# Expert blocks in one region of rows: full blocks of the first half, a mixed block an expert, then the rest

## What is computed

```
x = x + tanh(g_xattn[0]) * attention(layernorm(x), ctx)          # layer 1, 16 heads of 8
x = x + tanh(g_ffn[0])   * moe0(layernorm(x))                    # layer 2, the blocks of this change
x = x + tanh(g_xattn[1]) * bidaf_attention(layernorm(x), ctx)    # layer 3, called C here
x = x + tanh(g_ffn[1])   * moe1(layernorm(x))                    # layer 4, called D here

def moe0(x, Wg, W1, W2, W3):            # E = 8 experts, top 2
    top_w, top_i = top_k(x @ Wg, 2); top_w = softmax(top_w)
    y_e = (silu(x @ W1[e]) * (x @ W2[e])) @ W3[e]                # 128 -> 256 -> 128
    out = sum over the two chosen experts of top_w * y_e
```

## Time and profile before

| | |
|---|---|
| time, median of 3 runs | 523.1 us (522.99 to 526.55) |
| the profiled execution: its time, and the span of its trace | 524.74 us, 523.0 us |
| mean granted TensorE clock | 0.990 |
| busy: PE, DVE, ACT, POOL | 486.1, 401.3, 316.0, 230.5 us |
| stage A, B, C and D of the first and second half | to 212, to 354, to 523 us |
| blocks in stage B | 80 |

### The profile page before, as it was taken

The page is one execution under the profiler, slowest core; times in us unless marked ns, Lnnn a source line. Parts: engine busy times, 40 slices in busy tenths (PEclk is TensorE's granted clock), DMA queues, the critical chain, the costliest instruction groups (busy, mean ns, idle before and its releaser), DMA issues. The chain is left out here.

```text
span 523.0 us, 14426 instructions
## 1 busy us (share of the span) xinstructions
PE 486.1 (93%) x4456; PEld 395.8 (76%) x4456; DVE 401.3 (77%) x1582; ACT 316.0 (60%) x777; POOL 230.5 (44%) x316
## 2 busy tenths in 40 slices
PE   2688999999999999999999999989998999899997
PEld 1366777777777777777888887866897878779897
DVE  5788888888889878767756677676699895777973
ACT  1567887777887776455566655556553557453553
POOL 3322155555454554532450656532468863224420
PEclk9999999999999999899999999998999999998999
DMA  8703011111001220155664443320000112000011
GB/s 243 291 11 93 12 42 37 36 35 36 30 30 32 63 63 21 51 141 166 206 190 120 127 125 106 95 68 20 21 23 26 50 42 66 12 0 2 2 42 40
DMA packets 48130, 36.86 MB, mean 70 GB/s; under 512 B 6466, under 2 KB 43970, under 8 KB 47812
## 3 DMA queue, kind: packets, MB, share of 16 engines
q1 hardware_dynamic: 31332, 21.13, 13.5%
q0 software_dynamic: 4640, 9.45, 6.3%
q10 hardware_dynamic: 12096, 5.51, 3.8%
HBM read 22.44 MB, written 13.63 MB: 69 GB/s over the span
## 5 line engine op out<-in xcount | busy, mean ns | idle before, releaser
L468 POOL DMA_INDIRECT sent<-xr,rowu x60 | 59.8, 996 | 52.1 <-DVE rowu L1037 26.8
L484 POOL DMA_INDIRECT yg<-done,gidx x64 | 64.2, 1003 | 41.7 <-PE bank L1629 17.4
L1663 PE MATMUL bank<-QK 128*64 128x256 f32 x512 | 70.5, 397 | 8.4 <-ACT QK L612 5.4
L443 POOL TENSOR_TENSOR ve<-mv,half 128x4 f32<-128x4 f32 (+1 forms) x40 | 8.9, 222 | 114.8 <-DVE mv L833 113.8
L1234 DVE TENSOR_TENSOR act<-sil,bank 128x256 f32<-128x256 f32 x80 | 33.6, 420 | 33.4 <-ACT sil L674 33.0
L624 ACT ACTIVATE PT<-bank 128x512 f32<-128x512 f32 x64 | 36.4, 602 | 33.2 <-PE bank L1629 32.4
L674 ACT ACTIVATE sil<-bank 128x256 f32<-128x256 f32 x80 | 30.8, 385 | 38.7 <-PE bank L1819 38.3
L1663 PEld LDWEIGHTS bank<-QK 128*64 128x64 f32 x512 | 32.2, 139 | 27.0 <-ACT QK L612 6.8
L1835 PE MATMUL bank<-f0w_s,aT 128*128 x320 | 50.1, 279 | 0.9 <-DVE yb L1240 0.6
L912 DVE TENSOR_REDUCE mx<-bank 128x8 f32<-128x512 f32 x64 | 43.9, 686 | 8.5 <-PE bank L1663 8.4
L916 DVE TENSOR_TENSOR Pr<-bank,mx 128x512 f32<-128x512 f32 x64 | 43.7, 683 | 1.6
(11 more groups left out here) (241 smaller groups left out, 1294.3 us busy)
## 6 DMA issues: line engine op xcount, KB each, us to landing
xb<-sent SPq DMA_DIRECT2D x80, 64.0 KB
done<-yb ACTq DMA_DIRECT2D x80, 64.0 KB
cT<-ctx_t_dram SPq DMA_DIRECT2D x16, 128.0 KB, 2.2
f0w_s<-f_w_dram SPq DMA_DIRECT2D x1, 2048.0 KB, 11.0
Pr<-ctx_t_dram SPq DMA_DIRECT2D x8, 256.0 KB
QK<-ctx_tok_dram SPq DMA_DIRECT2D x8, 256.0 KB
out_dram<-xs SPq DMA_DIRECT2D x8, 256.0 KB, 2.3
xs<-x_dram SPq DMA_DIRECT2D x2, 512.0 KB, 5.6
```

The lines of the kernel that those rows point to most:

```text
L468: nc.gpsimd.indirect_dma_start(sent, bass.IndirectOffsetOnAxis(ap=rowu[:, s, 2 * k + c:2 * k + c + 1], axis=0), rows[:, c, :], None).then_ ...
L484: nc.gpsimd.indirect_dma_start(yg[:, s, j, :], None, done[u // (U4 // HALVES)], bass.IndirectOffsetOnAxis(ap=gidx[:, s, j:j + 1], axis=0)) ...
L1663: last = mm(bank[g % 2][L * b:L * (b + 1), 256 * p:256 * (p + 1)], QT[:, s, g, t:t + L], Kb[:, s, :, t:t + L], start=True, stop=True)
```

## The change

Both halves now send into one set of regions, and there is one list of `NB` = 64 + 8 - 1 = 71 blocks. The first `NBF` = 32 - 7 = 25 can only be full blocks of the first half and need only its rows. Then come the other full blocks of the first half, one mixed block for each expert (the rest of the first half and what follows of the second), and the rest of the second half. Results of the first half are all within blocks 0 to 39 (`NBH` = 40 stays as that bound).

- The table of the first 25 blocks is made in stage A, from counts rounded down. The table of the other 46 is made in steps 6 to 18 of stage B from sums over 24 runs of blocks (8 full, 8 mixed, 8 rest).
- `run` is no longer set anew for the second half. `zero_after` is gone from POOL; there is one set of 8 tails, written by SyncE, one in each of the steps t = 16 to 23 of its loop, after `first_of(t + 1)`.
- `half_sent(1)` stands ahead of block 25, not 40, and waits for the early spare blocks (8, were 16) and the 8 tails.
- The words of the second table are needed from `NW` = 16: by `load_word` at step 20.
- The sends of the last two units are tied to blocks 8 to 15.
- The context loads move from t = 10 to 40 to t = 22 to 52.
- The `back_...` work is over 16 thresholds in place of 8 experts, 32 x 16 = 512 elements, at steps 19 to 28, with a new `back_first` twice.
- Gathers are tied to `b_xt` >= 45 + 7 i / 8, at most 71; `comb` begins at t = 53 and takes a unit every 8 steps (56 and 9 before). The start of layer 3 is three steps nearer to the end of the loop.

```diff
-REGION = TOKENS // HALVES + P
+REGION = TOKENS + P
-NBH = 2 * TOKENS // HALVES // P + E
-NB = HALVES * NBH
-NW = NBH - 3
+PAIRS = 2 * TOKENS // P
+NB = PAIRS + E - 1
+NBF = PAIRS // HALVES - (E - 1)
+NBH = PAIRS // HALVES + E
+NW = NBF - PACK + 1
+NS = 3 * E
+TAIL = 16
+CTX = 22
+COMB = 53
...
             def half_sent(h):
-                sp.wait_ge(zeroed, 16 * E * HALVES)
-                sp.wait_ge(S("tails"), 16 * E * (h + 1))
+                if h == 1:
+                    sp.wait_ge(zeroed, 16 * E * 2)
...
+            def zero_after(e):
+                sp.wait_ge(S("tail"), 1)
+                r = sp.value_load(tail[0:1, e:e + 1], min_val=e * REGION, max_val=e * REGION + TOKENS)
+                sp.dma_start(sent[bass.ds(r, P), :], zero[:]).then_inc(zeroed, 16)
...
             for t in range(4, NB):
-                if t == NBH:
+                if t == NBF:
                     half_sent(1)
                     r = first_of(t)
                 sp.wait_ge(S("b_xt"), t - 3)
                 b_load(t, r)
-                if t + 1 < NB and t + 1 != NBH:
+                if t + 1 < NB and t + 1 != NBF:
                     r = first_of(t + 1)
-                if 10 <= t < 10 + 4 * U4 and t % 4 == 2:
-                    c_columns((t - 10) // 4)
+                if TAIL <= t < TAIL + E:
+                    zero_after(t - TAIL)
+                if CTX <= t < CTX + 4 * U4 and t % 4 == 2:
+                    c_columns((t - CTX) // 4)
...
-                        pool.wait_ge(S("b_xt"), NBH + 5 + 35 * (8 * u + j) // 32)
+                        pool.wait_ge(S("b_xt"), min(NBH + 5 + 7 * (8 * u + j) // 8, NB))
...
-            send(UA - 2, 0, (9, 11, 13, 15))
-            send(UA - 1, 1, (17, 19, 21, 23))
-            zero_after(1)
+            send(UA - 2, 0, (8, 9, 10, 11))
+            send(UA - 1, 1, (12, 13, 14, 15))
...
-            fetch(2, range(2))
             rstd(2, 0, 4)
-            fetch(2, range(2, 8))
-            fetch(3, range(1))
+            fetch(2, range(8))
             rstd(2, 1, 4)
-            fetch(3, range(1, 8))
+            fetch(3, range(8))
             rstd(2, 2, 4)
...
+                if t == 6:
+                    t_runs()
+                    t_run_rows()
+                if t == 9:
+                    t_run_steps()
                 if t == 11:
-                    t_count(1)
+                    t_all()
                 if t == 12:
-                    t_blocks()
-                    t_ends()
+                    t_rest()
                 if t == 13:
-                    t_owner(1)
-                    t_expert(1)
+                    t_rest_sums()
                 if t == 14:
-                    t_before()
-                    t_first(1)
-                if t == 17:
+                    t_rest_ends()
+                if t == 15:
+                    t_steps()
+                if t == 16:
+                    t_last()
+                if t == 18:
                     t_read(1)
-                if t == 18:
+                if t == 19:
+                    back_first(0)
+                if t == 20:
                     back_which(0)
-                if t == 19:
+                if t == 21:
                     back_shift(0)
-                if t == 20:
+                if t == 22:
                     back_row(0)
-                if t == 21:
+                if t == 23:
+                    back_first(1)
+                if t == 24:
                     back_which(1)
-                if t == 22:
+                if t == 26:
                     back_shift(1)
-                if t == 23:
+                if t == 28:
                     back_row(1)
...
-                    if t == 56 + 9 * u:
+                    first = COMB + 8 * u
+                    if t == first:
                         comb(u, 0, 0)
...
-                    if t == 61 + 9 * u:
+                    if t == first + 5:
                         moments(2, u, 4)
-                if t == 65:
+                if t == COMB + 7:
                     norm(0, 4, xn[:, 0], "c_ln", 2)
-                if t == NB - 9:
+                if t == NB - 6:
                     c_rmx(0)
...
-                if t == NB - 4:
+                if t == NB - 3:
                     norm(1, 4, xn[:, 1], "c_ln", 2)
+            moments(2, 2, 4)
...
-                if t == 16:
+                if t == 17:
                     t_row(1)
...
-                if t == NB - 12:
+                if t == NB - 9:
                     c_xt(0, 0)
-                if t == NB - 10:
+                if t == NB - 7:
                     c_s(0, 0)
                     c_own(0)
```

More of the change, by code:

```diff
@@ L80, in constants @@
     c[:, C_UP:C_UP + P] = p[:, None] < p[None, :]
[L81 to L85, removed]
+    c[:, C_RG:C_RG + E] = np.arange(E) * REGION
+    c[:, C_RC:C_RC + E] = np.arange(E) * REGION - (P - 1)
+    c[:, C_P] = p
+    c[:, C_RW] = p * P
+    c[:, C_RE] = E * REGION
+    c[:, C_ST:C_ST + NS] = np.where(np.arange(NS) % E == E - 1, 1 - E, 1)
     c[:, C_TR:C_TR + E * E] = (np.arange(E)[:, None] >= np.arange(E)[None, :]).reshape(-1)
@@ L395, in _ @@
                     sp.wait_ge(fill, 11)
[L396 to L399, removed]
+                    for e in range(E):
+                        r = E * REGION + P * e
+                        sp.dma_start(sent[r:r + P, :], zero[:]).then_inc(zeroed, 16)
             half_sent(0)
@@ L499, in body_a @@
                 send(u, s)
[L501 to L507, removed]
             with pool.Fori(0, E // 2) as i:
@@ L528, in returned @@
                 for k in range(4):
[L529 removed]
+                    stored = range(k, (NBH, NB)[h], 4)
+                    pool.wait_ge(st_b[k], 16 * len(stored))
             returned(0)
@@ L1053, in t_count, with t_full_blocks @@
                 stepped()
[L1054 to L1059 removed]
+            def t_full_blocks():
+                then(nc.vector.tensor_scalar(cnt[:], cnt[:], 7, None, ALU.logical_shift_right))
+                stepped()
+                then(nc.vector.tensor_copy(full[:], cnt[:]))
@@ new lines, in summed, with t_full_ends, t_owner @@
+            def summed(blocks):
+                stepped()
+                then(nc.vector.tensor_tensor(trn[:], blocks[:].unsqueeze(1).to_broadcast([P, E, E]),
+                                             cst[:, C_TR:C_TR + E * E].rearrange("p (e f) -> p e f", f=E), ALU.mult))
+            def t_full_ends():
+                summed(full)
+                stepped()
+                then(nc.vector.tensor_reduce(starts[:, 1:E + 1], trn[:], AX, ALU.add))
+            def t_owner():
+                stepped()
+                then(nc.vector.tensor_tensor(ge[:], cst[:, C_P:C_P + 1].to_broadcast([P, E]), starts[:, 1:E + 1], ALU.is_ge))
+                stepped()
+                then(nc.vector.tensor_reduce(ej[:], ge[:], AX, ALU.add))
```

192 lines of the change are left out of this document (114 added, 78 removed).

## The result

| | before | after |
|---|---|---|
| median of the runs that were compared, us | 523.82 (522.99 to 526.55) | 517.03 (515.37 to 518.04) |
| ratio, with its 95% interval | | 0.9854 (0.9825 to 0.9882) |
| the profiled execution: its time, the span of its trace, us | 524.74, 523.0 | 515.37, 513.6 |
| mean granted TensorE clock of that execution | 0.990 | 0.990 |

The change makes the kernel faster by 1.5%, 7.6 us by the ratio and 6.8 by the two medians, where 11.3 were forecast. The range of 508.8 to 518.0 holds the time, near its upper end; the range that the prediction gave to the sum alone, 509.5 to 514, does not. The two traces, both at a clock of 0.990, are 9.5 us apart (523.02 and 513.55).

A forecast was written before the change was run, and what follows sets the result against it. TensorE's own step was taken to bound the middle of stage B, with side work on top in outer steps. -13.6 + 1.1 + 0.5 + 0.7 = -11.3 us on 523.0 gave 511.7, median 511.8 us; range 508.8 to 518.0.

The forecast's parts named there:

- the sum alone: Whole kernel: all terms added, -11.3 us, giving 511.8 us; own range 509.5 to 514, chance 0.62.
- rival 1: Stage B, gate at block 25: load 2.4 us late, TensorE stands still, clock falls, 515.2 us; chance 0.14.
- nine blocks, and collisions at nothing: Stage B: nine blocks removed at 1.51 us each, -13.6 us; moved side work and its collisions 0.
- VectorE, steps 6 to 28: Stage B: side work beyond 0.45 us a step stands out, 2.0 us before and 3.1 after, +1.1 us.
- SyncE's queue and the gate: Stage B, steps 16 to 24 and block 25: slower queue shrinks the loads' lead; +0.5 us.
- gathers and the last steps: End of stage B: unit 3's gathers land late, holding VectorE's chain to `c_wrow`; +0.7 us, between 0 and 3.
- stage A: Stage A: POOL loses eight tails, VectorE four small instructions, beside a full TensorE; 0, at best -0.5 us.
- quiet step: Middle of stage B: a block step set by TensorE alone, 1.47 us with nothing else in it, priced at 1.51.
- the bound of the collisions: Stage B: moved `comb`, `sums`, `norm` and layer 3 start cost 0, between -1 and +1 us.
- the lead of 6.1 us: SyncE's queue at the start of the tail writes: four steps ahead less 0.3 us until the transpose signals.
- my 0.34 for the context load: SyncE's queue at t = 22: the context load takes 0.34 us off the lead of the block loads.
- the prediction's 512.3: Total if 64 KB transfers take the skill's 2.15 us, opening block 25's gate 0.45 us later; otherwise 511.8.

The follow-up runs named there:

- later roots: Changed kernel with the first three gathers of unit 3 ahead of rstd(2, 1) in GpSimd's queue: 514.48 us, ratio 0.9793 to the kernel before.
- the kernel with writes only: Changed kernel with tails on POOL and eight 64 KB writes to fixed spare places on SyncE, without register loads: 513.16 us, ratio 0.9809 to before.
- the kernel before with the added pairs: Kernel before plus eight register loads and 64 KB spare writes in SyncE's queue, t = 16 to 23: 529.18 us, ratio 1.0096 (first form 528.05 us).

## Why the prediction came out as it did

**Right in sign and main term; the queue's term too small and in another place, the end too small.** The measured 517.0 lies outside the sum's own range and nearest to rival 1 (515.2), which had a chance of 0.14. Term by term, in us:

| term | forecast | in the traces |
|---|---|---|
| nine blocks, and collisions at nothing | -13.6 | -15.0 |
| VectorE, steps 6 to 28 | +1.1 | +1.3 |
| SyncE's queue and the gate | +0.5 | +2.8 |
| gathers and the last steps | +0.7 | +0.8 as a wait, +2.0 with all behind it |
| stage A | 0 | -0.6 |

**The nine blocks** were priced right. The quiet step holds (1.47 or 1.48 us for most blocks in the middle after the change), and nine blocks put back cost 13.9 to 14.9 us. The -15.0 is 1.4 more than forecast, 0.4 beyond the bound of the collisions; what lies beyond the nine may be fewer collisions near the end, which I haven't taken apart.

**VectorE's steps** held: +1.3 from the kernel with the tails on POOL, in which no load is late, and spreading the `back_...` work over later steps gave 0.9 of it back. The sends and the context loads moved in the same stretch; no run changed them alone.

**SyncE's queue is the step that failed**, by its size: rival 1's mechanism came true, two blocks earlier than its place. I took 2.05 us a step from one register load (0.62) and one issue (0.43) on top of 0.96. The parts came to 2.20, and over blocks 16 to 23 the mean was 2.37, with one context load in it and one step (247.16) that started 0.35 later than its parts explain. So the lead of 6.1 us was down to about 1.8 at block 23, where my own pace and my 0.34 for the context load would have left 6.1 - 7 x 0.35 - 0.34 = 3.3. The second half of the error is the landing: 3.4 us where I bounded it by 1.7 to 2.5. With my lead, even 3.4 would have been late by no more than 0.1; with my landing of 1.7, the true lead would have sufficed by a hair. I had looked at the gate for the late load, and "loads of this queue in the same stretch never held TensorE before" is an argument about a queue that was not yet behind. By the fit of the Trainium skill (DMA: Bandwidth & Descriptors, Anatomy of one DMA), which the page gives for DMAs that GpSimd issues and the prediction used for SyncE's, 64 KB would take an estimated 2.15 us. The traces differ from it both ways: block 22's load took at most 1.9, block 23's 3.4, 3.2 and 3.3 in three traces. With 2.15 TensorE would have waited some 0.4 us. Nor does the prediction's 512.3 follow from that figure: a gate 0.45 later leaves block 25 a lead of 2.25, which still covers 2.15.

**The clock** was in rival 1 and not in the sum. Of the +2.8 us 1.7 are the wait and some 1.1 come after it (blocks 22 to 26 take 7.9 us, with the tails on POOL 6.8). It doesn't follow every time. Six traces have the wait of 1.6 to 1.9 us at block 23. In three (the changed kernel, later roots, nine more blocks) the clock in 256 to 262 us is 0.72 and blocks 22 to 26 take 7.8 to 7.9 us; in the other three it is 1.00 and they take 6.3. So the fall itself costs 1.6 us, and it came in half of these traces. The repetition of the changed kernel, behind its 1.9 us wait, ran at
```profile
256.00:262.00 6.00, 5.95 (x37) 4.86 (x37) 4.22 (x15) 3.11 (x11) 0.00 (x0) 1.00 0.57 168
```
The 0.72 of the first trace is a mixture of the two levels of 1.2 and 2.4 GHz. By the rule of the Trainium skill (TensorE: Matmul & The Clock Gate, Part 1) an idle array falls to half clock; the first trace agrees, the second has the same wait and no fall.

**The end** went by the mechanism forecast. The kernel after, VectorE's first sum of unit 3, the `wrow` that it holds up, POOL's roots, first and last gather, and TensorE's transpose of block 70 and wait for `wrow`, from the timelines, against the earlier trace rows:
```profile
345.00 1.14 DVE L1324 SCALAR_TENSOR_TENSOR xs<-yg,kept_w,xs 128x128 f32<-128x128 f32 x4 [1.28 <-DMA yg<-done,gidx]
...
331.35 0.20 POOL L468 TENSOR_TENSOR ve<-mv,half 128x4 f32<-128x4 f32 x1 [4.83 <-DVE mv L845]
...
333.72 1.04 POOL L509 DMA_INDIRECT yg<-done,gidx  x1 [0.75 <-issue]
...
342.56 0.94 POOL L509 DMA_INDIRECT yg<-done,gidx  x1 [0.30 <-issue]
...
335.99 0.27 PE L1712 MATMUL bank<-cst,xb 128*128 128x128 f32 x1
...
346.97 0.19 PE L1977 MATMUL bank<-cst,wrow 4*128 4x4 f32 x1 [1.23 <-DVE wrow L1373]
```
Unit 3 is summed 345.00 - 335.99 = 9.0 us after block 70, forecast 8.5. POOL had stood idle 4.83 us for the moments that its roots need, while gathers that needed none of it stood behind. TensorE's wait for `wrow` rose from 0.4 to 1.2 us: +0.8 for +0.7. The stretch behind the last block grew by 2.0, not 0.8, and that is no chance of one trace: it takes 173.8 to 177.8 us in the ten traces with the changed order and 171.7 to 173.5 in the three with the old one. One part is steady. The matmul that waits for `wrow` stands 8.9 to 9.1 us behind the last block's third pass where it stood 7.7, and 8.1 with the roots mended, so this term is about +1.2. The rest goes at least in part with the clock: in 348 to 358 us of the changed kernel it is 0.83, and the stretch from 10 to 20 us behind the last block has 0.83 or 0.66 in eight of the ten traces with the changed order and in one of the three with the old, 1.00 in the rest. Why the changed order has the fall more often stays open. `comb(0)` had no wait, as reckoned.

**Stage A** was costed at nothing, at best -0.5. I had said that a full TensorE covers POOL's tails there; it didn't. In the kernel before, POOL's tails and the roots behind them, and VectorE that waits for the roots:
```profile
183.86 0.54 POOL L507 DMA_DIRECT2D sent<-zero  x1 [0.60 <-issue]
184.41 0.21 POOL L443 TENSOR_TENSOR ve<-mv,half 128x2 f32<-128x2 f32 x1
...
185.66 0.62 DVE L844 TENSOR_SCALAR xr<-xs,ln 128x128 f32<-128x128 f32 x2 [1.60 <-POOL ln L446]
```
and in the kernel after, where POOL's roots come three microseconds earlier and nobody waits for them:
```profile
181.18 0.19 POOL L468 TENSOR_TENSOR ve<-mv,half 128x2 f32<-128x2 f32 x1 [3.45 <-DVE mv L845]
```
The transpose of block 0 begins at 212.3 to 212.7 us in the three kernels with tails in stage A and at 211.3 to 212.5, on the mean 211.7, in the ten without: about 0.7 us. No run changed this alone.

**Why the ratio gives 7.6 and the traces 9.5.** The changed kernel's other executions ran at 0.986 to 0.990 and took 516.97 to 518.04 us; the traced one had 0.990 and 515.37. The kernel before ran at 0.990 to 1.000. So the traced execution was the fastest of the four, while the one traced before the change lay above its median, and the difference of 9.5 is in part luck. That the stall at block 23 lowers the clock of the others is a guess: the changed kernel ran at 0.983 to 0.990 in eight of nine executions, but kernels with the same stall and one other edit ran at 0.987 to 0.993, about as the kernel with writes only (0.990 to 0.993), which has no stall. What made the changed kernel's own medians 2 to 3 us worse than these stays open.

## What to carry to other kernels

Where an in-order DMA queue is given more to issue, add up what one turn of it takes, register loads as well as issues, against the pace of its consumer, and follow the lead to the last turn in which it shrinks; a surplus of 0.7 us a turn was harmless for seven turns and then cost 1.7 to 2.8 us by the traces of the changed kernel, and 5 in the kernel before. Put small dynamic writes on a queue that is idle at that time, and put an instruction that waits for something late behind the independent work of its queue, not ahead of it. A unit of work that is removed is worth a quiet step, if its side work stays.

## What the runs showed of the hardware that was not expected

- A register load on SyncE took 0.62 us, the second one in a turn 0.70 up to the start of its write; the issue of a 64 KB DMA 0.34, and 0.2 to the next. Two pairs are 2.2 us, a pair and a write 1.6, a pair and a register load no more than 1.73.
- Block loads of 64 KB from the same queue were there within 1.9 us in one step and after 3.2 to 3.4 us in the next, with and without a context load near them; in the kernel before with the added pairs three in a row took 2.6, 2.7 and 3.6. Of the block loads that held TensorE back, each that took 3.0 us or more from issue to use had a 16 KB transfer of the kind `instruction`, 0.9 to 1.2 us long, within it.
- A wait of 1.6 to 1.9 us of TensorE was followed by a clock of 0.72 over 6 us in three traces and by 1.00 in three others, and executions of one kernel differ by 6 us with a clock of 0.984 to 0.999.
